# Cross attention: counting scores over a threshold on ScalarE, 24 segments, and four selections in a row

## The reference

```python
Q = (x_text @ Wq).reshape(Bb, Tt, H, DH)          # H = 4 heads, DH = 32
K = (x_vision @ Wk).reshape(Bb, Gg, H, DH)
scores = jnp.einsum('bthd,bghd->bhtg', Q, K) / np.sqrt(DH).astype(np.float32)
scores = jnp.where(vision_mask[:, None, None, :], scores, -jnp.inf)
topv, topi = jax.lax.top_k(scores, K_TOP)         # K_TOP = 32
probs = jax.nn.softmax(topv, axis=-1)
attn = jnp.zeros_like(scores).at[bi, hi, ti, topi].set(probs)
attn_mean = attn.mean(axis=1)
...
c_t = jnp.einsum('btg,bgd->btd', attn_mean, V)
```

## Time and profile before

| | |
|---|---|
| median of three runs | 4847.17 us |
| profiled execution | 4848.71 us, span of its core 4847.1 us, mean granted TensorE clock 0.895 |
| cross attention, first scan to last ranking | 1070.5 to 2376.7 us of the span |
| last ScalarE work of the stage | ends 2425.2 us |
| busy share over the whole span | PE 84%, PEld 68%, DVE 56%, ACT 30%, POOL 28% |

### The profile page before, as it was taken

How to read it: one execution, slowest core, us unless ns; L and a number is a source line. 1 busy time by engine, 2 the same in 40 slices (tenths; PEclk the granted TensorE clock), 3 DMA queues, 4 the chain that set the end, 5 groups by cost and what they waited for, 6 DMA issues and landing times. The chain is left out here.

```text
span 4847.1 us, 63484 instructions
## 1 busy us (share of the span) xinstructions
PE 4054.5 (84%) x20972; PEld 3313.9 (68%) x20972; DVE 2695.3 (56%) x8842; ACT 1434.8 (30%) x2211; POOL 1338.0 (28%) x1158
## 2 busy tenths in 40 slices
PE   6845899867877875678879799787999999999998
PEld 4722677636777774677768577665878777887786
DVE  8645455438989989989655455323434336222222
ACT  2354233235555544455400100222111112111111
POOL 0000111102121120121156324004667765432332
PEclk8668999977888887888889899897999999999999
DMA  1143322260010100100044422333122223000000
GB/s 57 36 146 113 108 84 87 74 201 29 18 53 15 44 30 7 44 30 11 6 153 142 145 83 104 144 120 123 61 64 72 72 61 104 29 20 20 27 24 18
DMA packets 248594, 336.94 MB, mean 70 GB/s; under 512 B 67524, under 2 KB 125764, under 8 KB 245958
## 3 DMA queue, kind: packets, MB, share of 16 engines
q1 hardware_dynamic: 151976, 177.79, 12.2%
q10 hardware_dynamic: 93744, 146.84, 8.9%
q0 software_dynamic: 2560, 8.39, 0.4%
HBM read 220.70 MB, written 112.25 MB: 69 GB/s over the span
## 5 line engine op out<-in xcount | busy, mean ns | idle before, releaser
L1621 PE MATMUL xa_ps_t<-xa_diag,xa_s_buf 128*128 128x128 f32 x4096 | 495.8, 282 | 144.2 <-DVE xa_s_buf L1808 74.3
L3053 DVE CAST m_act_hl<-m_g 128x512 fp32r<-128x512 f32 x256 | 139.7, 546 | 848.8 <-ACT m_g L2921 848.8
L1621 PEld LDWEIGHTS xa_ps_t<-xa_diag,xa_s_buf 128*128 128x128 f32 x4096 | 488.2, 198 | 162.4 <-issue 82.3
L1756 DVE MAX8 xa_cand<-xa_s_buf 128x8 f32<-128x64 f32 x4096 | 535.5, 217 | 83.5 <-ACT xa_s_buf L1667 67.4
L2747 POOL TENSOR_TENSOR m_act_hl<-m_g,m_act_hl 128x512 fp32r<-128x512 f32 x256 | 354.0, 1383 | 678.9 <-DVE m_act_hl L3053 678.9
L2921 ACT ACTIVATE m_g<-m_ps_h,m_b 128x512 f32<-128x512 f32 x256 | 176.2, 688 | 1117.0 <-PE m_ps_h L82 1111.9
L80 PE MATMUL m_ps_h<-m_hT,m_w 128*128 128x512 f32 x1024 | 416.9, 407 | 19.8 <-issue 17.8
L1556 POOL TENSOR_TENSOR xa_aT<-xa_a,xa_aT 128x512 fp32r<-128x512 f32 x128 | 159.8, 1270 | 984.2 <-ACT xa_a L1692 984.2
L82 PE MATMUL m_ps_h<-m_hT,m_w 128*128 128x512 f32 x1024 | 409.4, 400 | 0.0
L81 PE MATMUL m_ps_h<-m_hT,m_w 128*128 128x512 f32 x1024 | 409.1, 399 | 0.0
L80 PE MATMUL m_ps_o<-m_w,m_act_hl 128*128 128x512 f32 x1024 | 407.1, 398 | 0.7 <-POOL m_act_hl L2747 0.7
(11 more groups left out here) (373 smaller groups left out, 8179.4 us busy)
## 6 DMA issues: line engine op xcount, KB each, us to landing
at_xk<-in_x_dram SPq DMA_DIRECT2D x128, 128.0 KB, 2.7
spectrum<-df_yo ACTq DMA_DIRECT2D x32, 512.0 KB, 2.8
id_raw<-spectrum SPq DMA_DIRECT2D x32, 512.0 KB, 5.8
m_xt<-x ACTq DMA_DIRECT2D x64, 256.0 KB, 3.6
ky_raw<-in_ctx_dram SPq DMA_DIRECT2D x16, 768.0 KB, 6.3
xa_ks<-kt SPq DMA_DIRECT2D x48, 256.0 KB
xa_raw<-in_ctx_dram SPq DMA_DIRECT2D x32, 384.0 KB, 3.3
w<-bf_out_t SPq DMA_DIRECT2D x32, 256.0 KB, 2.5
```

Source lines behind the costliest of these rows:

```text
L1621: last = pe.matmul(ps_t[:, c // 4, c % 4, :], s_buf[:, t % 2, h, k0:k0 + P], diag[:, h, :], start=(h == 0 and c % 4 == 0), stop=(h == HEAD ...
L1756: dve.max(out=ranks[h][:, :, g], in_=s_buf[:, t % 2, h, g * SEG:(g + 1) * SEG])
```

## The change

`stage_cross` now cuts the scores into 24 segments of 85 or 86. The marks and their sums are gone: ScalarE runs over the scores of tile t again (`counts`), takes the sign of score minus threshold and adds these up per row, and TensorE adds the rows up with a column of ones (`sum_counts`). The slow path is taken only where more than 32 scores of a row really reach the threshold. The denominators are the accumulator outputs of the four selections, which now stand in one row on VectorE, with two diagonals behind each pair. All scans of tile t+1 stand before the selections of tile t. raw has three buffers, the context's pieces are spread differently, and SyncE's first loads no longer wait for GpSimd's constants.

```diff
-    SEGS = 32
-    SEG = S2 // SEGS
+    SEGS = 24
+    EDGES = [S2 * g // SEGS for g in range(SEGS + 1)]
+    SETTLED = (2 * TOPK - S2) * P * HEADS
...
-        raw = sb("raw", [P, 2, 2, DV])
+        raw = sb("raw", [P, 3, 2, DV])
...
@@ sync: keys, start, context
+                    if b == 0:
+                        sp.wait_ge(s_zero, h + 1)
                     sp.dma_start(ks[96:97, h, :].bitcast(F32), km_in[b:b + 1, :]).then_inc(s_ks[h], 16)
...
-                sp.wait_ge(s_const, 3)
                 queries(0)
...
@@ gpsimd
-                pool.memset(ks[96:128, :, :].bitcast(F32), 0.0)
                 pool.memset(qs[96:128, :, :, :].bitcast(F32), 1.0)
                 pool.drain().then_inc(s_const, 1)
+                for h in range(HEADS):
+                    pool.memset(ks[96:128, h, :].bitcast(F32), 0.0)
+                    pool.drain().then_inc(s_zero, 1)
...
@@ tensor
-                def sum_rows(t):
...
-                def sum_flags(t):
...
+                def sum_counts(t):
+                    if t == 0:
+                        pe.wait_ge(s_const, 3)
+                    pe.wait_ge(s_cnt, HEADS * (t + 1))
+                    if t >= 1:
+                        pe.wait_ge(s_chk, t)
+                    pe.matmul(ps_f[:, 0:HEADS], ones[:, :], count[:, :], start=True, stop=True)
+                    for h in range(HEADS):
+                        last = pe.matmul(ps_f[:, HEADS:HEADS + 1], ones[:, :], count[:, h:h + 1], start=(h == 0), stop=(h == HEADS - 1))
                     last.then_inc(s_f, 1)
...
                         pe.wait_ge(s_sel, HEADS * t + h + 1)
+                    if half == 0 and h % 2 == 0:
+                        pe.wait_ge(s_diag, 2 * t + h // 2 + 1)
                     if h == 0:
-                        pe.wait_ge(s_diag, t + 1)
...
                 def mix(t):
-                    pe.wait_ge(s_aTl, 4 * t + 4)
...
                     for c in range(GC):
+                        if c % 4 == 0:
+                            pe.wait_ge(s_aTl, 4 * t + c // 4 + 1)
...
@@ scalar
-                def denominators(t):
...
+                def counts(t, h):
+                    act.wait_ge(s_cand, t + 1)
+                    if t >= 1 and h == 0:
+                        act.wait_ge(s_sel, HEADS * t)
+                    if h >= 2:
+                        act.wait_ge(s_cnt, HEADS * t + h - 1)
+                    act.activation(prob[:, h % 2, :], s_buf[:, t % 2, h, :], ACT.Sign, bias=under[:, t % 2, h:h + 1],
+                                   accum_out=count[:, h:h + 1]).then_inc(s_cnt, 1)
...
                 def exponentials(t, h):
                     act.wait_ge(s_chk, t + 1)
-                    for h in range(HEADS):
-                        act.activation(e_top[:, h, :], ...
-                    if t >= 1 or h >= 2:
+                    if h >= 2:
                         act.wait_ge(s_sel, HEADS * t + h - 1)
...
@@ vector: rank, settle, select, diagonals
-                    dve.tensor_tensor(flags[:, :, :, :], cand..., ALU.is_ge)
+                    lowest = top[:, k, :, TOPK - 1]
+                    dve.tensor_scalar(under_a[:, :], lowest, -(1.0 - 2.0 ** -23), 1e-30, ALU.mult, ALU.add)
+                    dve.drain()
+                    dve.scalar_tensor_tensor(out=under[:, k, :], in0=lowest, scalar=-(1.0 + 2.0 ** -23), in1=under_a[:, :],
+                                             op0=ALU.mult, op1=ALU.max)
...
-                    with dve.If(doubt > P * TOPK * HEADS):
+                    with dve.If(doubt > 0):
...
-                                             op0=ALU.is_ge, op1=ALU.mult).then_inc(s_sel, 1)
+                                             op0=ALU.is_ge, op1=ALU.mult, accum_out=den[:, h:h + 1]).then_inc(s_sel, 1)
...
+                def diagonals(t, h):
+                    dve.drain()
+                    dve.reciprocal(rec[:, h:h + 2], den[:, h:h + 2])
+                    dve.drain()
+                    if t >= 1:
+                        dve.wait_ge(s_dg, 8 * t - 2 + h)
+                    dve.tensor_scalar(diag[:, h, :], ident[:, :], rec[:, h:h + 1], None, ALU.mult)
+                    dve.tensor_scalar(diag[:, h + 1, :], ident[:, :], rec[:, h + 1:h + 2], None, ALU.mult).then_inc(s_diag, 1)
...
                     if more:
-                        scan(t + 1, 0, 0, 24)
+                        scan(t + 1, 0, 0, SEGS)
+                        scan(t + 1, 1, 0, SEGS)
+                        scan(t + 1, 2, 0, SEGS // 2)
...
                     if more:
-                        scan(t + 1, 1, 0, SEGS)
+                        scan(t + 1, 3, 0, SEGS)
                     if t >= 0:
-                        diagonals(t)
                         select(t, 0)
                         select(t, 1)
-                    if more:
-                        scan(t + 1, 2, 0, SEGS)
-                    if t >= 0:
+                        diagonals(t, 0)
                         select(t, 2)
                         select(t, 3)
+                        diagonals(t, 2)
                     if more:
-                        scan(t + 1, 3, 0, SEGS)
                         rank(t + 1)
```

More of the change, by code:

```diff
@@ L1433, in stage_cross @@
         top = sb("top", [P, 2, HEADS, TOPK])
-        to_head = sb("to_head", [P, HEADS, HEADS + 1], BF16)
-        f_weight = sb("f_weight", [NW, 2])
-        f_sums = sb("f_sums", [NW, 2, HEADS + 1])
+        ones = sb("ones", [P, 1])
+        under = sb("under", [P, 2, HEADS])
+        under_a = sb("under_a", [P, HEADS])
+        count = sb("count", [P, HEADS])
         flag_i = sb("flag_i", [1, HEADS + 1], mybir.dt.int32)
         nmax = sb("nmax", [P, 2, HEADS])
-        e_top = sb("e_top", [P, HEADS, TOPK])
         den = sb("den", [P, HEADS])
@@ L1450, in stage_cross @@
         ps_ac = psum("ps_ac", [P, DV])
-        ps_f = psum("ps_f", [P, 3, HEADS + 1])
+        ps_f = psum("ps_f", [1, HEADS + 1])
         s_const = sem("constants")
-        s_raw = [sem(f"raw_loaded{k}") for k in range(2)]
+        s_zero = sem("mask_rows_zeroed")
+        s_raw = [sem(f"raw_loaded{k}") for k in range(3)]
         s_chi = sem("ctx_hi")
@@ L1516, in _ @@
                 queries(1)
-                context(0, 0)
-                context(0, 1)
+                for g in range(3):
+                    context(0, g)
                 for t in range(TILES):
@@ L1525, in _ @@
                             keys(b + 1, h)
-                        context(b + 1, 0)
-                        context(b + 1, 1)
+                        for g in range(3):
+                            context(b + 1, g)
                     if t % TPB == 0:
-                        for g in range(2, 8):
+                        for g in range(3, 8):
                             context(b, g)
@@ L1545, in _ @@
                                    base=0, pattern=[[-1, P]], channel_multiplier=1).then_inc(s_const, 1)
[L1546 to L1551, removed]
+                pool.memset(ones[:, :], 1.0)
                 pool.drain().then_inc(s_const, 1)
@@ L1724, in _ @@
                         mixed(t - 1)
-                    if t + 1 < TILES:
-                        copy(t + 1, 3)
-                    if t % TPB == 0:
-                        for g in range(4):
-                            context_hi(t // TPB, g)
+                    b, new = t // TPB, t % TPB == 0
+                    if new:
+                        context_hi(b, 0)
+                        context_hi(b, 1)
+                    if new:
+                        context_hi(b, 2)
+                        context_hi(b, 3)
                     hi(t, 0)
+                    if new:
+                        context_hi(b, 4)
                     hi(t, 1)
+                    if new:
+                        context_hi(b, 5)
                     if t + 2 < TILES:
                         copy(t + 2, 0)
-                    if t % TPB == 0:
-                        for g in range(4, 8):
-                            context_hi(t // TPB, g)
+                    if new:
+                        context_hi(b, 6)
                 hi(TILES - 1, 2)
```

100 lines of the change are left out of this document (39 added, 61 removed).

## The result

The changed kernel takes 4867.10 us (median of 5, 4865.19 to 4869.83) against 4846.77 (4844.12 to 4849.34): ratio 1.0043, 95% interval 1.0030 to 1.0055, so 20 us slower, where 41 were forecast. The profiled execution took 4865.19, its span 4863.5; the profiled executions of the two kernels lie 16.5 us apart, and all that is read from traces adds up to that difference.

What follows compares the result with a forecast made beforehand. VectorE was taken to bound the kernel, a ring through all engines after the change. Periods +132, start -11, slow path -47 and context -33 sum to +41: 4888 us on the median, range 4840 to 4935.

Steps and rivals of the forecast that it cites:

- the ring: Attention stage: a dependence chain once round all engines' in-order lists sets the tile period, 41.5 us where 37.6 stands.
- the plain periods: Attention stage tiles without slow path or context pieces: 42.0 us each, 4.4 more than before; +132 over 30 periods.
- the context: Context pieces in the attention stage: three buffers and spreading them among ScalarE's work save 33 us, 10 left.
- Start: Stage start: queries and keys go out 9.3 us earlier; with the shorter last scan and ranking, -11 us.
- slow path: Heads flagged in the attention stage: one (tile 17, head 1) instead of three, -47 us.
- steps 1 to 4 and 7: First turns 3.73 us, copies 2.21, second turns with scores 8.2, ScalarE's copies and counts 9.6; selections with diagonals 10.9.
- steps 5 and 6: Five tiny matmuls plus conversion, 0.9 us; then half of scan 2, sum load and branch (0.40), scan 3: 5.9.
- The clock addition of 0.5 a tile: TensorE's clock falling after a pause of about 1.9 us between first-half turn pairs: 0.5 us a tile added.
- the rival that the clock falls for the second turns in every tile: TensorE's second-half turns: 3.5 to 7 us more, 45 to 48.5 a tile, 4980 to 5085 us; chance 0.06.
- the rival of the table: Concerns ScalarE loading an activation table in this stage; the prediction as given states no size or chance.
- all terms end in the stage: Whole program: every term falls in the attention stage, which a barrier ends, so all count in full.
- The rival "VectorE sets the pace": Attention stage: VectorE's shorter list sets the period, 34.5 to 39 us a tile, 4665 to 4800 us; chance 0.10.

Runs made afterwards that it cites:

- cut_ctx: ring_cut with the context pieces spread further on ScalarE, GpSimd's list following; 4799.37 us.
- before_pad: Kernel before the change with one tiny fp32 matmul a tile more, the first of sum_flags issued twice; 4825.48 us, ratio 0.9955.
- ring_cut: Kernel after with head 1's scores of the tile after next put between the second-half turns of heads 1 and 2 on TensorE; 4801.01 us.
- segs32: Kernel after with 32 segments in place of 24; 4866.43 us.

## Why the prediction was right, and where not

The mechanism of the stage was right: the ring is there, and its steps are the ones that were named. That the stage's sum came out so near, +38 for +41, is luck in part: the plain periods cost 21 us less than forecast and the context gave back 20 us less, and the two cancel. Start and slow path came to within 2 us. Ring: 41.17 for 41.5; steps 1 to 4 and 7 came within 0.2. Only steps 5 and 6 were too long, by 0.25 and 0.3: the load of the sum shows no 0.40 gap here, scan 3 follows scan 2 without one. The clock addition of 0.5 a tile was not paid: the turns of a plain tile run at a granted clock of 1.00, 3.81 a pair. These two are the 0.8 a tile between 42.0 and 41.17. So the rival that the clock falls for the second turns in every tile did not come; ScalarE loads an activation table at 0.9 and 3355.2 us and never in this stage, so the rival of the table fell too, and one head was flagged, as forecast.

Mis-sized was the context term: 31 us are left where I estimated 10, since I had counted the pieces' own durations on ScalarE only. Followed round the ring tile by tile, about 9 of them are the mix, which waits for piece 7:

```profile
1489.50 0.69 PE L80 MATMUL xa_ps_ac<-xa_ctx_hl,xa_aT 128*128 128x384 f32 x1 [5.47 <-POOL xa_ctx_hl L1557]
```

About 8 are diagonals on VectorE that take five to six times as long while GpSimd subtracts pieces beside them. One of a plain tile, the second pair of the ninth stretch, and GpSimd beside these:

```profile
1329.89 0.29 DVE L1826 TENSOR_SCALAR xa_diag<-xa_ident,xa_rec 128x128 f32<-128x128 f32 x1
...
1454.06 1.41 DVE L1826 TENSOR_SCALAR xa_diag<-xa_ident,xa_rec 128x128 f32<-128x128 f32 x1
1455.39 1.84 DVE L1827 TENSOR_SCALAR xa_diag<-xa_ident,xa_rec 128x128 f32<-128x128 f32 x1
...
1451.64 7.27 POOL L1557 TENSOR_TENSOR xa_ctx_hl<-xa_raw,xa_ctx_hl 128x768 fp32r<-128x768 f32 x3 [9.50 <-ACT xa_ctx_hl L1702]
```

In after eight diagonals start while such a subtraction runs. They take 1.40 to 1.84 us, and each ends 0.08 us behind the end of the subtraction; the other 120 take 0.28 or 0.29. That they wait for GpSimd is read from these ends; no run moves GpSimd's work alone. TensorE waits longer before the turns behind them, 2.65 us for 1.59, and their clock is 0.68:

```profile
1457.37 5.36 PE L1620 MATMUL xa_ps_t<-xa_diag,xa_s_buf 128*128 128x128 f32 x32 [2.65 <-DVE xa_diag L1827]
```

Slower turns of this kind make about 7 of the 31 us, pieces between the copies about 3. The last 4 or 5 are pauses of VectorE that stand in other tiles for the most part (below). Moving the pieces in cut_ctx took 7.5 us away and gave 6.1 back at two other steps; what sets off each fall of the clock is not settled. Nor is the tail's 3 us.

The step that failed is the sentence that all terms end in the stage, which put the rest of the program at nothing: it left out that 64 fewer matmuls and weight loads on TensorE (20908 for 20972) move all its code behind, which was worth 23 us. Against before_pad (0.9955), whose FFN stage runs without the pauses, the kernel after (1.0043) is 42 us slower, close to the forecast; so 4867 for 4888 is, in the main, the right mechanism less a gain that the change did not aim at. The rival "VectorE sets the pace" named the right remedy, head 1's scores not behind the second turns, but a period of 38.85 came of it, and VectorE, busy for 32.56 of it, still waits 2.18 us for copy 0 and 2.51 for the sum there: it does not set the pace.

## What to carry to other kernels

When work moves between engines with in-order lists, follow one dependence once round all lists and add starts to starts: that ring, not the busiest engine, can be the period, and its cheapest cut may be one matmul group issued earlier. Compare two kernels stage by stage before explaining a difference: a stage that nobody touched can move by more than the change itself. If a loop shows pauses with no releaser where a pass begins, count the instruction fetches there and shift the code (here by 128 instructions) before believing any gain or loss.

## What the runs showed of the hardware

The place of TensorE's code alone is worth 22 us in the FFN stage: four pauses of about 4 us with 35 more instruction fetches (62 for 27), and a granted clock of 0.50 to 0.75 in the 4 us behind each. Where the pauses are missing, q8 is silent through the second and third pass of both loops.

A small instruction on VectorE can last until the one that GpSimd has under way ends: a diagonal took 1.40 to 1.84 us for 0.28, eight times in after. That it waits for GpSimd is argued from the ends. MAX8 does not show it: the ranking's row at 1457.32 takes its usual 0.84 us beside the same subtractions.

VectorE shows smaller pauses with no releaser. In after, at 1440.31, 1932.88 and 2061.75, they are 0.43, 0.61 and 1.87 us, in ring_cut 0.47, 0.64 and 1.23 in the same tiles:

```profile
1440.31 3.52 DVE L1761 MAX8 xa_cand<-xa_s_buf 128x8 f32<-128x85 f32 x23 [0.43 <-issue]
```

In segs32, whose VectorE list is longer, none stands in the ninth stretch. This fits fixed places of the code; no run tests it for itself.
